# Straight code in place of register loops, and a new order of steps, in a DLRM interaction tower

## The reference

```python
combined = jnp.concatenate([dense_features[:, None, :], sparse_features], axis=1)
interactions = jnp.einsum('bnd,bmd->bnm', combined, combined)
interactions_flat = interactions[:, _TRIU_I, _TRIU_J]
...
h = jnp.concatenate([z, r_dense_features], axis=1)
h = jnp.maximum(h @ W_top1 + b_top1, 0.0)
h = jnp.maximum(h @ W_top2 + b_top2, 0.0)
y = h @ W_top3
```

## Time and profile before

| | us |
|---|---|
| median of three timed runs | 425.25 |
| the three runs | 422.16, 425.25, 428.37 |
| span of the profiled execution | 631.9 |
| time of that execution around its span | not given |
| TensorE busy in the span (matmuls) | 404.1 |
| VectorE, ScalarE, GpSimd busy | 222.2, 198.5, 281.3 |

### The profile page before, as it was taken

How to read it: one execution, slowest core, us unless ns; L and a number is a source line. 1 busy time by engine, 2 the same in 40 slices (tenths; PEclk the granted TensorE clock), 3 DMA queues, 4 the chain that set the end, 5 groups by cost and what they waited for, 6 DMA issues and landing times.

```text
span 631.9 us, 14126 instructions
## 1 busy us (share of the span) xinstructions
PE 404.1 (64%) x6097; PEld 357.1 (57%) x6097; DVE 222.2 (35%) x216; ACT 198.5 (31%) x286; POOL 281.3 (45%) x293
## 2 busy tenths in 40 slices
PE   2620774625966487842887568674486946968677
PEld 2610663624856375832777556574475835858566
DVE  4631454514533152412334144140351414534221
ACT  2410223222434142420244214232041421435523
POOL 6777427372535437360272625546046362630000
PEclk9775678777878679875697758896579866879878
DMA  5642102212111122012020121111212012110010
GB/s 133 189 154 55 35 23 57 79 51 78 38 36 38 45 75 56 23 46 75 15 56 22 47 82 35 48 29 47 64 26 56 26 46 77 38 32 32 28 56 1
DMA packets 22371, 33.91 MB, mean 54 GB/s; under 512 B 8300, under 2 KB 15036, under 8 KB 22310
## 3 DMA queue, kind: packets, MB, share of 16 engines
q0 software_dynamic: 9248, 18.93, 11.6%
q1 hardware_dynamic: 13062, 14.04, 6.8%
HBM read 29.30 MB, written 3.68 MB: 52 GB/s over the span
## 4 chain that ended last, share of the span: by engine, by line
PE 53%; issue 24%; another core or an unknown queue 11%; ACT 5%; DMA 3%; DVE 2%; SPq 1%; ACTq 0%; DVEq 0%
PE hot_ps L566 21%; PE gram_ps L590 12%; PE transpose_ps L543 4%; PE mlp_ps L613 4%; PE mlp_ps L603 3%; PE mlp_ps L601 3%; PE mlp_ps L602 3%; DMA embed_t<-table 3%; ACT embed_t L385 2%; PE hot_ids_ps L548 1%; DVE one_hot L460 1%; ACT embed_t L348 1%; ACT hidden_hi L360 1%; DVE table_lo L464 0%
## 5 line engine op out<-in xcount | busy, mean ns | idle before, releaser
L322 POOL DMA_INDIRECT rows<-table,ids_sb x288 | 280.4, 974 | 277.2 <-PE transpose_ps L543 176.5
L566 PE MATMUL hot_ps<-one_hot,table_hi 125*128 125x256 f32 x512 | 170.7, 354 | 71.4 <-ACT embed_t L385 53.5
L460 DVE TENSOR_TENSOR one_hot<-hot_ids_ps,row_numbers_sb 125x1024 fp32r<-125x1024 f32 x128 | 156.2, 1233 | 129.1 <-remote 68.1
L566 PEld LDWEIGHTS hot_ps<-one_hot,table_hi 125*128 125x128 f32 x512 | 122.2, 239 | 79.4 <-issue 38.6
L566 PE MATMUL hot_ps<-one_hot,table_lo 125*128 125x256 f32 x512 | 158.2, 330 | 3.5 <-issue 3.5
L590 PE MATMUL gram_ps<-embed_t 128*27 128x27 f32 x4096 | 79.8, 213 | 118.5 <-issue 113.9
L590 PEld LDWEIGHTS gram_ps<-embed_t 128*27 128x27 f32 x4096 | 63.1, 125 | 137.7 <-issue 133.3
L566 PEld LDWEIGHTS hot_ps<-one_hot,table_lo 125*128 125x128 f32 x512 | 123.2, 241 | 4.3 <-issue 4.3
L348 ACT COPY embed_t<-transpose_ps 128x512 f32<-128x512 f32 (+1 forms) x80 | 92.8, 1160 | 81.0 <-remote 43.0
L446 DVE COPY_PREDICATED units<-late_sb,gram_ps 128x208 f32<-128x208 int32 x32 | 34.8, 1089 | 159.8 <-ACT units L379 159.6
L385 ACT COPY embed_t<-hot_ps 128x256 f32<-128x256 f32 x64 | 44.4, 694 | 81.0 <-PE hot_ps L566 41.5
(11 more groups left out here) (40 smaller groups left out, 242.7 us busy)
## 6 DMA issues: line engine op xcount, KB each, us to landing
rows<-table,ids_sb POOLq DMA_INDIRECT x288
embed_t<-table SPq DMA_DIRECT2D x8, 500.0 KB
bounce<-units SPq DMA_DIRECT2D x8, 448.0 KB, 2.5
scratch<-bounce SPq DMA_DIRECT2D x7, 378.0 KB
rows<-dense SPq DMA_DIRECT2D x16, 64.0 KB
scratch<-w SPq DMA_DIRECT2D x1, 512.0 KB
scratch<-w_units SPq DMA_DIRECT2D x2, 252.0 KB
rows<-bounce SPq DMA_DIRECT2D x1, 378.0 KB
```

The source lines that it names most:

```text
L322: nc.gpsimd.indirect_dma_start(rows[:, t2, f, :], None, tables[table], bass.IndirectOffsetOnAxis(ids_sb[:, slot, table:table + 1], 0)).the ...
L460: nc.vector.tensor_tensor(one_hot[:, half], ids_over, numbers_over, ALU.is_equal).then_inc(one_hot_ready, 1)
L566: last = nc.tensor.matmul(hot_ps[:, 0:GROUP], table[:, k, step, :], one_hot[:, half, j, :], start=(step == 0 and table is table_hi), stop= ...
```

## The change

The five register loops become Python loops, so that all eight groups stand written out on each engine, with constants in waits and addresses. In both lists of `STEPS` the gram rounds G0 and G1 now come first, and Q0 to Q4 each follow one lookup; H12 to H15 have one transpose part among them. `LAST_STEPS` and `FIRST_STEPS` are as before. SyncE waits for `mlp_copied` ahead of the second transfer of pack, that is until all seven results of the group before have been copied. The two unread counters are gone.

```diff
 STEPS = [
-    "B0 G0 H0 H1 Q0 G1 H2 Q1 H3 S0 Q2 H4 Q3 H5 W0 M0 H6 W1 M1 Q4 M2 H7 W2 M3".split(),
-    "G0 H8 M4 H9 Q0 M5 H10 Q1 H11 M6 H12 Q2 H13 W3 Q3 H14 W4 Q4 H15 G1".split(),
+    "B0 G0 G1 H0 Q0 H1 Q1 H2 Q2 H3 Q3 S0 H4 Q4 H5 W0 M0 H6 W1 M1 M2 H7 W2 M3".split(),
+    "G0 G1 H8 Q0 M4 H9 Q1 M5 H10 Q2 H11 Q3 M6 H12 Q4 H13 W3 H14 W4 H15".split(),
 ]
...
-        gathers_begun = sem("gathers_begun")
-        rounds_begun = sem("rounds_begun")
...
                 sp.wait_ge(units_stored, 16 * (g + 1))
 
+                if landing is packed_raw:
+                    sp.wait_ge(mlp_copied, MLP_USES * g + 1)
                 by_row = bounce.rearrange("(s n) x -> s (n x)", s=BLOCK)[:, 0:N * UNITS * GROUP_BLOCKS]
...
-            with sp.Fori(1, GROUPS // 2 - 1) as i:
+            for i in range(1, GROUPS // 2 - 1):
...
-                if not first:
-                    pool.sem_inc(gathers_begun, 1)
                 for u in range(TILE_BANKS):
                     if not first:
 
                         pool.wait_ge(transposed, TILE_BANKS * (SLOTS * i + slot - TILES) + u + 1)
-                        pool.sem_inc(gathers_begun, 1)
...
-            with pool.Fori(1, TILE_COUNT // SLOTS) as i:
+            for i in range(1, TILE_COUNT // SLOTS):
...
-            with act.Fori(0, GROUPS // 2 - 1) as i:
+            for i in range(GROUPS // 2 - 1):
...
-                dve.sem_inc(rounds_begun, 1)
...
-            with dve.Fori(0, GROUPS // 2 - 1) as i:
+            for i in range(GROUPS // 2 - 1):
...
-            with pe.Fori(0, GROUPS // 2 - 1) as i:
+            for i in range(GROUPS // 2 - 1):
```

## The result

The changed kernel takes 432.45 us (median of 4 runs, 430.26 to 435.32), the kernel before, beside it on the same chip, 425.18 us (422.16 to 428.37). The ratio is 1.0174, 95% interval 1.011 to 1.0239: slower, though the interval does not decide whether by 2%, where I had forecast 416.5 us and faster.

A forecast was written before the change was run, and what follows sets the result against it. TensorE was taken to set the end by little, with GpSimd the limit just below. Loops -15.2 and lost cover +6.6 gave -8.6, so 425.25 became 416.6, rounded 416.5 us; range 404 to 430.

The forecast's parts named there:

- Loops written out: TensorE's two jumps back: straight code takes away 7.6 us of waiting at each, 15.2 us for both.
- Two gram rounds first: G0 and G1 paired in each tile's step: stalls of 3.9 us a group become 3.2 to 4.5, taken as 0.
- clock term: Bounded by -14 and +14 us, and let cancel the bare lookups H13 to H15 (3.9) and H2 (2.7).
- rival (2): Pairs stall and leave the clock low for the next lookups, 4.5 us a group: slower, put at 434 us; chance 0.12.
- rival (3): Everything helps: low clock gone from the first tile (-14 us), gathers never wait, 405 us; chance 0.13.
- What lost its cover: At group borders B0 G0 follows H15 and waits for ScalarE's copy: 0.94 us in seven groups, +6.6 us.
- Transposes early: Transpose parts beside lookups, releasing gathers earlier: taken as 0, with -4 us as the other end.
- SyncE's wait: Added wait ahead of pack's second transfer: 0; if cover failed, 2.6 + 4.6 us a group on the cast.
- floor of 406 us: GpSimd's 288 unbroken gathers, 366.9 us, plus 3.25 ahead and 35.9 for the last products; not expected to be reached.
- Rival (1): GpSimd is already the bound, so only the rest of the wait can go: 421 us; chance 0.27.
- Rival (4): Pauses belong to the blocks, not the jump, so straight code keeps them and the hop is added: 432 us; chance 0.03.
- reading of the span: The profiled span of 631.9 us against 425.25 timed was taken mostly as waits of the profiled execution only.

The follow-up runs named there:

- e11: The changed kernel (straight code, SyncE's new wait) with both lists of steps as before the change: 408.52 us, ratio 0.9617 to the kernel before.
- e14: The kernel before, loops kept, with the new lists of steps and SyncE's new wait: 458.01 us, ratio 1.0788.
- e13: The changed kernel with G1 moved behind the second lookup in both lists, early transposes kept: 408.09 us, ratio 0.9635.
- e8: The changed kernel without the gathers of tiles 2 to 15, TensorE reusing the rows of the first two tiles: 431.51 us on a 425 chip.
- e10: The kernel of e11 with the first tile's G1 put directly behind G0: 424.33 us, ratio 1.0017.
- e9: The kernel of e11 without the gathers of tiles 2 to 15: 392.01 us, ratio 0.9229.

## Why the prediction was wrong

**Loops written out, -15.2: the mechanism right, the size partly by luck.** e11 is 15.3 us under the kernel before on its chip and 16.7 under the one measured with the change. But e11 stands on the floor that the gathers set and waits 8.5 us for rows, and in the new order, where nothing of that kind holds TensorE up, the loops cost 26 us: two jumps of 7.6 us are not all that they cost. The rows that it was read from, were of a 640 chip, and the jump's stall is the same on both (8.67 and 8.64 there, 8.25 in e14). The pauses of 4 to 5 us at the borders are gone from e11 and from the kernel after. What the sum calls fetches are the waits of the earlier trace rows. Straight code does not end every wait for instructions: 0.86 to 2.20 us of idle time stand at the ends of blocks inside the pairs shown above.

**"Two gram rounds first", taken as 0 (bounds -5 to +4): the step that failed.** The measured price is 432.45 - 408.5 = 24 us (the two ratios, 1.0174 and 0.9617, give the same), 3.4 a group; against e13, which has no pairs, that is 1.7 us for each of the 14. The gathers' floor under e11 and e13 hides a part, so it is the least that the pairs cost. The sum for the old order was wrong first: the earlier trace rows gave 1.61 us for the pair at the border and 2.27 for the round behind it, 3.9 a group. These rows lie behind the last gather, where 215 matmuls run in 2.28 us and use up a block sooner. Amid the gathers, on a 425 chip, the same two places stall 1.15 and 0.52 us, 1.7 together. For the new order I had 3.2 to 4.5 a group. Stalls at the ends of blocks are 28.6 / 8 = 3.6 us a group in the kernel after and 12.8 / 8 = 1.6 in e11. So "after" was right, and "before", with 3.9, was over 2 us a group too dear. What I had missed is that a stall belongs to a block and not to a round: the pair makes sure that one whole block is gram. Of the 26.0 us between the two spans 20.3 are idle time ahead of gram (37.8 against 17.5), some 15 of these are such stalls and some 4 the hop below. Another 7.7 us are busy time of TensorE (349.5 against 341.8), 5.0 are idle time ahead of lookups, and against that stand the 8.5 us for which e11 waits for rows.

The busy time is the clock term, which I had let go both ways (-14 to +14) and let cancel 3.9 + 2.7 us in the sum, and of which rival (2) has 2 us a group and rival (3) all 14. No row before the change and no run shows a term of 14 us, or of 2 a group. The runs show this: behind the pair at 144.55, which stalls twice, the granted clock is 0.50, and a matmul of a lookup takes 0.215 us; the earlier trace rows have 5.53 / 26 = 0.213 at 0.57 and 9.93 / 85 = 0.117 at 0.98. The pair at 195.57 stalls once by 0.86 and keeps 1.00; behind the one at 240.77, which stalls once by 1.96, 19 matmuls take 3.40 us at 0.50. The lookups' busy time is 148.4 + 138.8 us after and 145.6 + 135.9 in e11, 5.7 us more, 0.8 a group: the sign of the rival, and less than half of its 14.

**"What lost its cover", +6.6: there, about 4 us, and hidden where the gathers rule.** TensorE idles 0.69 us (0.80 at the last) ahead of the round at each of the six borders between groups from 144.5 on. The releaser reads "issue", but the gap stands only in kernels in which B0 G0 follows H15. In the kernel after it is on TensorE's path. e13 has it too (0.69 at 132.17) and stands at 408: there it goes under in what the gathers allow.

**Transposes early 0, SyncE's wait 0: right on a 425 chip**, by e13 and e11. In the kernel after the casts of the packed units have 0.0 us of idle time ahead of them, and the wait of the earlier trace rows never turns up. (e11 and e13 stand on the gathers' floor, so a small cost would not show in their times.) The floor of 406 us was right to 2.5 us: 408.5 and 408.1 are the times at which the gathers run unbroken from 3 us to 370 and two products remain.

**The rivals.** It was rival (2), put at 0.12, in its kind: a stall in each pair, and the low clock behind some. Its full price was 4.5 us a group with 2.2 as the point from which it decides; 3.4 were measured. That its 434 lies beside the measured 432.45 is luck: it was a figure set between 441 and 426, its pair term was only 0.6 us a group because "before" was too dear, and its low clock twice a group did not come. Rival (1), GpSimd as the bound, is true of e11 and e13 and false of the kernel after, although the sign that I had named for it (pauses gone, gathers unbroken, time not less) is there; e8 tells them apart. Rival (4) named 432 as well, but its pauses went with the jumps.

**The reading of the span.** I took 631.9 against 425.25 as the profiler's doing. A run of the kernel before on a 640 chip takes 632 to 644 us without it. The error cost no term by itself, but it led me to take the price of a gram round from the stretch behind the gathers as the "clean" one, which was no nearer to the measured chip than the rest.

Shown by the runs: the gain of straight code, the loss by the second round beside the first (e10, e13), and that it does not need the gathers (e8, e9). That the stall is a wait for the next block of instructions rests on its place in the stream and on the transfer ahead of it, in every one of these kernels; in e8, where the same matmuls take 42.9 us and not 56.5, the idle time ahead of them is larger (43.4 us), as it must be when blocks are used up sooner. No run moved the ends of the blocks alone, with the same order of steps; what comes nearest is that they lie otherwise from pair to pair within one kernel, as at 144.55 and 195.57. Open: what sets the start of a block's transfer, why two kinds of chips treat one kernel so differently, and whether early transposes of the first tile cost 4% on the one.

The straight code in the old order beats both kernels wherever it ran: 0.9617 on a 425 chip, 0.940 and 0.9429 on the two 640 chips. e13 is its equal on a 425 chip.

## What to carry to other kernels

Write out a loop whose body is long for TensorE: here two jumps back cost at least 15 us of 425, and the stall rows at the jumps (8.25 to 8.67 us each) give most of the price. Where runs of very small matmuls wait for instructions, as the gram rounds did here, keep them apart with larger matmuls: here every block of 256 instructions that was gram from end to end ended in a stall of 0.7 to 2.5 us, and where the granted clock fell to 0.50 behind it, a matmul of a lookup took 0.215 us in place of 0.12. Two lookups between two rounds were not enough where both rounds nearly filled a block. Price such a stall at a place with the same neighbours and the same pace as the one that you change, and when profile and timing disagree by half, find out first whether they are of the same chip.

## What the hardware showed that I had not expected

- One program takes 424 to 426 us on some chips and 632 to 644 on others. The gathers make nearly all of the difference: without most of them the changed kernel takes 431.5 and 451.5 us.
- The stall at a jump back is the same in both orders (8.64 and 8.67 us, 8.25 in e14), yet the loops cost 15 to 17 us in the old one and 26 in the new one: TensorE's lower granted clock (0.890 against 0.919) adds to it in the new one, and the wait for gathered rows (8.5 us in e11) cuts the gain short in the old.
- Every stall inside the gram rounds of the straight kernels on a 425 chip stands 193 instructions past a multiple of 256 and ends 1.2 to 1.6 us after a block of 16,384 bytes of instructions has been transferred.
- The granted clock was 0.50 behind a pair with 4.3 us of stalls in 7.85 us, and stayed 1.00 behind one with 0.86 in 4.83.
- A pause of 1.02 us between two rounds left a stall of 0.55 in one tile's step, and one of 1.33 us came on top of a stall of 2.29 in the other's: some 12 us slower in all.
